# One more store queue, five engines that clear, and two operations in another order: a four-part edit of a state-space and mixture-of-experts block on one core

## The reference

```python
x = x + L0_xattn(ctx, layernorm(x))     # state-space scan, result gated by silu(layernorm(x))
x = x + L0_ffn(layernorm(x))            # 16 experts, top 4 of each token, beside a shared expert
x = x + L1_xattn(ctx, layernorm(x))     # a second state-space scan with other weights
x = x + L1_ffn(layernorm(x))            # ternary weights, activations rounded to 8 bits

def step(state, inp):                   # the scan, 16 states per channel, 512 channels
    d, b, c, u = inp
    state = state * exp(d[..., None] * A) + (d * u)[..., None] * b[:, None, :]
    return state, einsum('bdn,bn->bd', state, c)
y = (y + D[None, :, None] * u) * silu(z)        # z is layernorm(x), transposed

def _qlinear(x, w):                     # L1_ffn: gate and up 512 -> 2048, down 2048 -> 512
    wq, ws = clip(round(w / mean|w|), -1, 1), mean|w|
    s = max|x| / 127 + 1e-5
    return (clip(round(x / s), -128, 127) @ wq.T) * s * ws
out = _qlinear(silu(_qlinear(x, w_gate)) * _qlinear(x, w_up), w_down)
```

## Time and profile before

| | |
|---|---|
| device time, 3 runs | 2117.39, 2118.13, 2119.98 us |
| the profiled execution's own time | 2118.25 us |
| its span | 2116.4 us |
| granted TensorE clock, mean | 0.90 |
| busy: PE / DVE / ACT / POOL | 1618.6 / 1715.7 / 1169.4 / 1330.6 us |
| third block ends, clear, fourth block starts | 1802.1, 1802.3 to 1806.7, 1806.9 us |

### The profile page before, as it was taken

One profiled execution on the slowest core, in us unless ns is written; L12 is line 12 of the kernel. 1 busy time (PEld: TensorE's weight loads), 2 busy tenths in 40 slices (PEclk: granted clock), 3 DMA queues, 4 the chain that ended last, 5 costly groups with the idle time before them and its releaser, 6 DMA issues. The chain is left out here.

```text
span 2116.4 us, 26823 instructions
## 1 busy us (share of the span) xinstructions
PE 1618.6 (76%) x8338; PEld 916.9 (43%) x8338; DVE 1715.7 (81%) x2270; ACT 1169.4 (55%) x1798; POOL 1330.6 (63%) x645
## 2 busy tenths in 40 slices
PE   4675765766664558888888898999999999067788
PEld 1222222322224435666566555666655665023344
DVE  3999999999967656998599947888658887678876
ACT  5676776676643116655666535455354444146576
POOL 2689878788973002998099915888418887654221
PEclk7788988889986569999999999999999999579999
DMA  6646546446547122432333243545445642642200
GB/s 212 231 160 229 203 144 217 161 149 197 179 139 267 63 76 89 142 120 78 120 115 105 89 173 132 186 155 199 152 156 180 230 142 77 197 121 61 74 16 31
DMA packets 130517, 305.19 MB, mean 144 GB/s; under 512 B 23856, under 2 KB 33328, under 8 KB 126288
## 3 DMA queue, kind: packets, MB, share of 16 engines
q1 hardware_dynamic: 86800, 206.33, 28.8%
q10 hardware_dynamic: 32144, 59.65, 8.0%
q0 software_dynamic: 11440, 37.50, 6.0%
HBM read 215.09 MB, written 88.34 MB: 143 GB/s over the span
## 5 line engine op out<-in xcount | busy, mean ns | idle before, releaser
L494 POOL TENSOR_TENSOR ssm_hs<-ssm_hs,ssm_Cs 128x1024 f32<-128x1024 f32 x128 | 313.9, 2464 | 90.6 <-DVE ssm_hs L461 90.6
L494 POOL TENSOR_TENSOR moe_hs<-moe_hs,moe_Cs 128x1024 f32<-128x1024 f32 x128 | 301.6, 2356 | 48.9 <-DVE moe_hs L461 48.0
L461 DVE TENSOR_TENSOR_SCAN moe_hs<-moe_dA,moe_bu 128x1024 f32<-128x1024 f32 x128 | 292.5, 2285 | 21.1 <-ACT moe_dA L375 13.0
L484 POOL TENSOR_TENSOR moe_U<-moe_U,moe_hs 128x1024 f32<-128x1024 f32 x128 | 301.9, 2359 | 6.4
L1446 PE MATMUL moe_pgu<-all_Wreg,moe_xt 128*128 x1896 | 301.0, 312 | 0.0
L461 DVE TENSOR_TENSOR_SCAN ssm_hs<-ssm_dA,ssm_bu 128x1024 f32<-128x1024 f32 x128 | 291.5, 2278 | 0.1
L294 PE MATMUL ssm_pY<-ssm_hs,ssm_ident 128*128 128x512 f32 x512 | 278.4, 671 | 8.1 <-POOL ssm_hs L494 7.9
L1396 PE MATMUL moe_pgu<-all_Wreg 128*128 128x256 f16 x2112 | 250.9, 276 | 13.9 <-DVE moe_hsl L1647 13.9
L1396 PEld LDWEIGHTS moe_pgu<-all_Wreg 128*128 128x128 f16 x2112 | 208.9, 99 | 62.1 <-issue 13.7
L1446 PEld LDWEIGHTS moe_pgu<-all_Wreg,moe_xt 128*128 128x128 f16 x1896 | 185.4, 98 | 94.7 <-issue 2.3
L747 POOL TENSOR_TENSOR ssm_wlo<-ssm_wst,ssm_whi 128x1360 f16<-128x1360 f32 (+2 forms) x63 | 188.5, 2991 | 34.1 <-ACT ssm_wst L682 34.1
(11 more groups left out here) (272 smaller groups left out, 3212.1 us busy)
## 6 DMA issues: line engine op xcount, KB each, us to landing
ssm_wst<-in_w_all SPq DMA_DIRECT2D x51, 680.0 KB, 5.2
y_d<-moe_yo ACTq DMA_DIRECT2D x79, 256.0 KB
all_Wreg<-w_hi SPq DMA_DIRECT2D x16, 1088.0 KB
all_Wreg<-w_lo SPq DMA_DIRECT2D x16, 1088.0 KB
w_hi<-ssm_whi SPq DMA_DIRECT2D x51, 340.0 KB, 2.3
w_lo<-ssm_wlo SPq DMA_DIRECT2D x51, 340.0 KB, 3.1
ssm_Cs<-c_d SPq DMA_DIRECT2D x64, 256.0 KB, 5.5
moe_Cs<-c_d ACTq DMA_DIRECT2D x64, 256.0 KB, 3.9
```

The lines of the kernel that those rows point to most:

```text
L461: self.nc.vector.tensor_tensor_scan(self.hs[:, j, :, :].rearrange("p k t -> p (k t)"), self.dA[:, q, :, :].rearrange("p k t -> p (k t)"), ...
L484: self.nc.gpsimd.tensor_tensor(Y, Y, self.hs[:, j, :, :], ALU.add).then_inc(self.acc_done, 1)
L494: self.nc.gpsimd.tensor_tensor(self.hs[:, j, :, :], self.hs[:, j, :, :], self.Cs[:, i:i + 1, :].to_broadcast([P, HC, L]), ALU.mult)\
```

## The change

Four edits.

**A.** The store of the last batch's y is issued by SyncE, ahead of its wait for the landing, and no longer by ScalarE.

**B.** `Mem.clear` gives each of the five engines every fifth semaphore.

**C.** In the fourth block, GpSimd multiplies pieces 0 and 2 of the first batch by the gate and VectorE pieces 1 and 3. For this VectorE's work on the experts' results of tile 4 is cut in pieces that stand around it.

**D.** `x_transpose(i+1)` stands behind the third product of a tile (and its `h_transpose(i-1, 1)`), no longer behind the fourth; `x_evac(i+1)` stands behind the third product's Silu, `h_evac` and gates, ahead of the fourth Silu.

```diff
@@ Mem.clear
             @block.sync
             def _(sp):
-                for s in self.sems:
+                for s in self.sems[0::5]:
                     sp.sem_clear(s)
+            @block.scalar
+            def _(act):
+                for s in self.sems[1::5]:
+                    act.sem_clear(s)
...            (the same for vector [2::5], tensor [3::5], gpsimd [4::5])
@@ experts_and_ssm, SyncE
                     last_weights(rows)
+                S.store_y(sp, y_ssm, B - 1)
                 sp.wait_ge(S.y_dram, 16 * B)
@@ experts_and_ssm, ScalarE
                     y_evac(g)
                     y_store(g)
-                S.store_y(act, y_ssm, B - 1)
@@ tail, GpSimd
-                for i in range(KC):
+                for i in range(0, KC, 2):
                     y_gate(i)
@@ tail, VectorE
                 norm(0, 0, c_sd, c_rs, c_ln)
-                combine(KC)
+                dve.wait_ge(y_in[0], 16)
+                for k, i in enumerate(range(1, KC, 2)):
+                    weighted(KC, k)
+                    dve.wait_ge(g_rdy, i + 1)
+                    V.tensor_tensor(Y[:, 0, i, :], Y[:, 0, i, :], G[:, 0, i, :], ALU.mult).then_inc(yg_rdy, 1)
                 for i in range(KC):
                     gated(i)
                 norm(1, 0, a_sd, a_rs, a_ln)
+                weighted(KC, 2)
                 x_scale(0)
                 dve.wait_ge(xr_rdy, 1)
                 V.tensor_scalar(xq[:, 0, :], xn[:, 0, :], -ROUND, 127.0, ALU.add, ALU.min).then_inc(xq_rdy, 1)
                 x_scale(1)
+                weighted(KC, 3)
+                combined(KC)
                 combine(KC + 1)
@@ tail, ScalarE
                         for j in gate_at(b, t, f):
                             gate_of(j)
+                        if f == 2 and i + 1 < TT:
+                            x_evac(i + 1)
                         if f == 3 and i + 2 < TT:
                             layernorm(i + 2)
-                    if i + 1 < TT:
-                        x_evac(i + 1)
@@ tail, TensorE
                         if i and f in (1, 2):
                             h_transpose(i - 1, f - 1)
+                        if f == 2 and i + 1 < TT:
+                            x_transpose(i + 1)
                         if b + 1 < B and (t, f) in GATED:
                             y_transpose((b + 1) * KC + GATED[t, f])
-                    if i + 1 < TT:
-                        x_transpose(i + 1)
```

More of the change, by code:

```diff
@@ L101, in _ @@
             def _(sp):
-                for s in self.sems:
+                for s in self.sems[0::5]:
                     sp.sem_clear(s)
+            @block.scalar
+            def _(act):
+                for s in self.sems[1::5]:
+                    act.sem_clear(s)
+            @block.vector
+            def _(dve):
+                for s in self.sems[2::5]:
+                    dve.sem_clear(s)
+            @block.tensor
+            def _(pe):
+                for s in self.sems[3::5]:
+                    pe.sem_clear(s)
+            @block.gpsimd
+            def _(pool):
+                for s in self.sems[4::5]:
+                    pool.sem_clear(s)
 class Ssm:
```

## The result

The changed kernel takes 2112.7 us (median of 14 runs, 2107.6 to 2119.4), the kernel before 2119.8 in 14 runs beside it (2114.3 to 2125.7). The ratio is 0.997 (95% interval 0.996 to 0.998): faster by 0.3%. I had forecast 2112.0 from 2118.25, a ratio of 0.9970. The profiled execution's span is 2110.2 us, 6.2 less than before. (One run of the kernel of experiment 5 fell in a slower state, 2867.6 us at a granted clock of 0.55, and is left out of its median.)

The account below looks back on a forecast made before the run. No engine bounds the whole span; block ends, clears, fourth block's start and FFN were read separately. -0.9 - 5.6 - 1.0 + 1.3 = -6.2 from 2118.25 gives 2112.0 us, range 2106.5 to 2115.5.

Parts of the forecast that it names:

- A, -0.9: Third block's end: y's store lands sooner, GpSimd's DRAIN then ends the block, saving 0.9 us.
- rival 1: Third block's end: GpSimd's DRAIN is no bound and y's landing sets it; -2.2 to -2.9 us, total 2110.4; chance 0.14.
- B, -5.6: Three semaphore clears: five engines side by side at 0.12 us a clear take 4.4 us instead of 10.0.
- C, -1.0: Fourth block's start: gate multiplications split between GpSimd and VectorE end at 1841.0 instead of 1841.9, gaining 1.0 us.
- That costs nothing, because the second one waited 2.87 us for the Silu: Tile 0: VectorE's put-off work moves the first gate multiplication from 1859.65 to 1859.8, hidden by the second's Silu wait.
- rival 2: Tile 0: the 3.1 us before the second Silu were an accident and vanish; 1.6 us more gain, 2110.4; chance 0.20.
- D, +1.3: Fourth block's tiles: early evacuation costs 0.57 in tile 4 and 0.9 in tiles 7, 8, 10; tiles 0, 1 gain 0.1.
- From tile 12 on TensorE is full and the transposes only change their place: Fourth block's last tiles: TensorE is busy throughout, so moving the transposes adds nothing; tiles 12 to 14 stay 34.7 us.
- My +0.3: Fourth block: net of the gate split's -1.0 us and the next input's earlier handling, +1.3 us.
- Rival 4: Fourth block's tiles: early evacuation makes ScalarE and VectorE wait for GpSimd's clip and TensorE's transposes; 2123 us; chance 0.04.
- the 1.0 us of slack: Steady tiles: clip(13) ends at 2065.4, 1.0 us before the moved transposes' new place at 2066.4.
- Rival 3: No measurable change: clears give only -4.0, the gate -0.6, the next input's move costs +2.5; 2115.3 us; chance 0.16.

Follow-up runs that it names:

- experiment 5: Changed kernel with edit C taken back, so GpSimd does all four first-batch gate multiplications: 2119.28 us, ratio 0.9979 to the kernel before.
- experiment 2: Changed kernel with edit A taken back, so ScalarE issues y's last store again: 2114.85 us, ratio 0.9981 to the kernel before.
- experiment 3: Changed kernel with edit D taken back, next input's transposes and evacuation at their old places: 2111.7 us, ratio 0.9966 to the kernel before.
- experiment 4: Changed kernel with half of edit D: next input's transposes stay early, ScalarE's evacuation returns behind the fourth Silu; one run, 2118.76 us.
- experiment 10: Changed kernel with SyncE clearing semaphore ranges by single instructions and edit D kept in tile 0 alone: 2107.01 us, ratio 0.9945 to the kernel before.

## Why the prediction was right, and where only its sum was

**A, -0.9.** Right in size and reason. GpSimd's DRAIN is next in line, and rival 1, that y's landing sets the end, fell twice (rows above, experiment 2). The Trainium skill ("VectorE: DVE Perf Modes", "The DRAIN you can't avoid") gives its constant of about 12 ns for the DRAINs of a program's preamble and postamble. At the end of the third block SyncE's 7 and ScalarE's 8 ns agree with it, and GpSimd's 8920 behind its indirect DMAs doesn't. Reading that constant for the ends of blocks too would have been the mistake, and the prediction went by the row instead.

**B, -5.6.** Measured -5.4. The pitch on TensorE is 117 ns where I had taken 120 between 57 and 171. Nothing in the rows singled it out, so that was fortune; 57 ns would have given -7.7. The forecast set 4.4 us against 10.0, from the first clear to the last; to the next block's start it is 5.35 against 10.8.

**C, -1.0.** The first half was right: TensorE's transposes came 1.3 us sooner (my sum in turns with overlap gave 1.0), with the slowed instructions that were expected. The exclusive lock of the Trainium skill ("SBUF — State Buffer", "🔬 SBUF: two separate sides") would have left 0.6 by strict turns; the measured 1.3 is on the other side of my value, so the two engines overlap more here than full blocking allows. The second half failed, the step "That costs nothing, because the second one waited 2.87 us for the Silu". The wait belongs to some executions only. Without it VectorE is the bound of tile 0 at once, the put-off 1.6 us of weighting and statistics comes ahead, and of the 1.3 us 0.2 to 0.4 are left. I had named the accident as rival 2, with 0.20, but hung my own term on the wait as well; seven of thirteen profiles have it.

**D, +1.3.** The wrong term. (Its own terms, 0.57 + 0.9 - 0.1, make 1.4.) It was +2.9 from tile 7's scale to the end (114.8 us against 111.9), made of three pieces. The 0.6 us in tiles 8 to 10 is the Silu held up by the evacuation, which I had at 0.2 to 0.4 a tile. In tile 4 the fourth Silu does come 0.58 us later against its third (3.65 for 3.07), as forecast, but the tile's length moved by 0.03. Tile 4 takes 16.6 us or more at a clock of 0.79 or 0.80 in all six profiles with the whole of D, and 15.3 at 0.89 in four of the seven others, so D may cost 1.3 us more there by the clock; two profiles without D have 16.6 as well, and it isn't shown. What tile 7 paid can't be told either.

The step that failed is "From tile 12 on TensorE is full and the transposes only change their place". A busy share of 34.70 in 34.70 with modelled ends doesn't mean that TensorE waits for nobody. The ring goes product 3, Silu, multiplication, scale, rounding, clip, multiplication of product 0, product 2 of the next tile, and it was as long as TensorE's own work to within 0.02 us (product 2 at 0.47 where TensorE is ready at 0.45). The moved transposes lengthen it by their 0.22: 4 x 0.23 = 0.9 us, which experiments 3 and 4 show.

The third piece is the clock: TensorE's last `down` took 4.8 to 5.3 us in all seven profiles with D's early transposes in every tile, and 3.6 in five of the six others, 5.06 in the sixth. So 1.2 to 1.7 us go with D in these profiles, and not with it alone; why the clock falls there more often I can't say. All of this is read from traces, one for each kernel: the runs with and without D don't differ clearly (experiment 3).

**The sum.** In the pair of profiles the fourth block is 0.8 us shorter: tile 0 -2.9 (the late Silu gone, C), tiles 1 to 7 -0.7 (tile 1 -1.3, tile 7 +0.5; their clock, as far as can be seen, since experiment 10 finds nothing of D in tile 1), the rest +2.9. My +0.3 was the sum of two terms that were both off, and the late Silu, which I had carried over unchanged, made up for it. Over the runs the forecast 2112.0 stands beside 2112.7.

**Rival 4**, a wait for GpSimd's clip in each tile, can be seen once: in tile 0 TensorE stands 1.3 us for it (1858.10 in the changed kernel). In the steady tiles the transposes follow those of h with no gap, and the 1.0 us of slack was enough. Rival 3 was wrong on the pitch.

## What to carry to other kernels

Between blocks look at the number of instructions first: 167 clears cost 10.8 us on one engine, 5.4 on five, and 1.25 as four instructions over a range, while the store that seemed to hold the block gave 0.9. Work that is moved ahead on a "full" engine may lie in a ring through other engines, and then costs its whole length each time; compare the start of each product with the end of what it waits for, not with the busy share. A wait that covers a put-off piece should be seen in more than one profile before the cover is counted on.

## What was not expected of the hardware

- GpSimd's DRAIN takes about 83 ns for each indirect DMA that it has issued since the last DRAIN, though all have long landed: 0.14 us for one, 0.37 for four, 5.3 for 64, 6.5 for 79.
- A semaphore clear costs 55 to 57 ns on SyncE, 67 on ScalarE, 71 on GpSimd, 84 on VectorE and 117 on TensorE, start to start; one over a range of numbers 63 to 122 ns on SyncE.
- In seven of the thirteen profiles the signal of tile 0's second product comes 2.3 to 4.3 us behind the end that the profile gives it (which is modelled), 55.0 to 57.9 us into the fourth block, and the third product's signal follows 0.1 us later. ScalarE is idle meanwhile, and VectorE for a part of it. TensorE's clock rises to its upper level near there, at 50.1 to 54.0 us, but it does so in the six others too. What TensorE does there stays open.
